# Four cross-attention layers on one core: narrower matmul tiles and one step order per engine

## The reference, cut to what matters

```python
# layer 0: 64 channels, 256 positions; no heads, 1x1 convolutions
Mn, Mm = Wn @ norm(x) + bn, Wm @ norm(ctx) + bm
A = softmax(Mn.T @ Mm)                    # 256 x 256 per batch
x = Wo @ ((Wl @ ctx + bl) @ A.T) + bo + x
# layers 1 and 2: 16 heads of 16, 64 queries and 64 keys per batch
a = layer_norm(ctx) * gamma + beta
Q, K, V = x @ Wq.T, a @ Wk.T, a @ Wv.T    # scores * 16 ** -0.5, masked
x = x + tanh(gate) * (softmax(Q K.T) V) @ Wo.T
# layer 3: one head of 256
x = x + alpha * (softmax((x Wq.T) (ctx Wk.T).T / 16) (ctx Wv.T)) @ Wo.T
```

## Time and profile before

| | us |
|---|---|
| median of 3 runs | 635.41 (635.09 to 635.55) |
| the profiled execution | 634.87 |
| its span | 633.1 |
| PE busy | 602.1 (95%) |
| ACT busy | 478.2 (76%) |
| DVE busy | 467.6 (74%) |
| POOL busy | 119.1 (19%) |

### The profile page before, as it was taken

The page is one execution under the profiler, slowest core; times in us unless marked ns, Lnnn a source line. Parts: engine busy times, 40 slices in busy tenths (PEclk is TensorE's granted clock), DMA queues, the critical chain, the costliest instruction groups (busy, mean ns, idle before and its releaser), DMA issues.

```text
span 633.1 us, 22469 instructions
## 1 busy us (share of the span) xinstructions
PE 602.1 (95%) x9203; PEld 540.0 (85%) x9203; DVE 467.6 (74%) x1036; ACT 478.2 (76%) x929; POOL 119.1 (19%) x136
## 2 busy tenths in 40 slices
PE   1899999999999999999999999999999999999995
PEld 1688998889898898989988898988989899889884
DVE  4866778686885869767786868858697677867474
ACT  0998779776885959857797768859598577977682
POOL 3602330107010060103301070100601033000000
PEclk9999999999999999999999999999999999999999
DMA  5420002010021000210020100210002100001001
GB/s 160 147 72 2 3 3 72 3 35 2 2 74 34 2 2 4 71 34 2 2 72 2 35 2 2 72 35 2 1 5 71 35 2 1 3 2 36 1 3 34
DMA packets 18486, 18.10 MB, mean 29 GB/s; under 512 B 1828, under 2 KB 18340, under 8 KB 18404
## 3 DMA queue, kind: packets, MB, share of 16 engines
q1 hardware_dynamic: 18024, 16.55, 8.2%
q0 software_dynamic: 320, 0.26, 0.2%
q10 hardware_dynamic: 60, 0.01, 0.0%
HBM read 12.63 MB, written 4.19 MB: 27 GB/s over the span
## 4 chain that ended last, share of the span: by engine, by line
PE 85%; ACT 5%; DVE 4%; issue 2%; DMA 1%; SPq 1%; DVEq 0%; POOL 0%; ACTq 0%; POOLq 0%
PE psum L401 13%; PE psum L403 10%; PE psum L402 10%; PE psum L641 10%; PE psum L716 10%; PE psum L662 8%; PE psum L709 4%; PE psum L629 4%; PE psum L507 2%; PE psum L467 2%; PE psum L532 2%; PE psum L515 2%; PE psum L546 1%; DMA mrow_u<-in_mask_dram 1%; PE psum L652 1%
## 5 line engine op out<-in xcount | busy, mean ns | idle before, releaser
L1046 DVE TENSOR_TENSOR shifted<-psum,negmax 128x512 f32<-128x512 f32 x128 | 88.5, 691 | 9.7 <-ACT work L842 4.8
L842 ACT ACTIVATE work<-shifted 128x512 f32<-128x512 f32 x128 | 78.1, 642 | 20.0 <-DVE shifted L1046 19.7
L1042 DVE TENSOR_REDUCE negmax<-psum 128x8 f32<-128x512 f32 x128 | 87.3, 682 | 4.7 <-PE psum L641 4.5
L856 ACT ACTIVATE work<-psum,group_mask 128x512 f32<-128x512 f32 x128 | 79.4, 697 | 2.1 <-PE psum L662 1.7
L641 PE MATMUL psum<-kbd,work 64*128 64x128 f32 x1024 | 69.7, 280 | 0.6 <-issue 0.4
L662 PE MATMUL psum<-const,work 64*128 64x64 f32 x1536 | 65.3, 225 | 4.3 <-ACT work L835 1.1
L716 PEld LDWEIGHTS psum<-v,work 128*64 128x64 f32 x2048 | 62.4, 138 | 6.8 <-issue 5.4
L662 PEld LDWEIGHTS psum<-const,work 64*128 64x128 f32 x1536 | 57.5, 139 | 10.6 <-issue 7.7
L641 PEld LDWEIGHTS psum<-kbd,work 64*128 64x128 f32 x1024 | 61.9, 188 | 5.2 <-issue 3.3
L716 PE MATMUL psum<-v,work 128*64 128x34 f32 x2048 | 66.1, 225 | 0.0
L803 ACT ACTIVATE work<-psum,const 128x512 f32<-128x512 f32 x64 | 40.5, 684 | 25.0 <-PE psum L403 24.8
(11 more groups left out here) (184 smaller groups left out, 1609.8 us busy)
## 6 DMA issues: line engine op xcount, KB each, us to landing
x_raw<-in_x_dram SPq DMA_DIRECT2D x8, 512.0 KB, 4.0
c_raw<-in_ctx_dram SPq DMA_DIRECT2D x8, 512.0 KB, 4.9
out_dram<-attn SPq DMA_DIRECT2D x16, 256.0 KB, 2.3
mrow_u<-in_mask_dram SPq DMA_DIRECT2D x8, 64.0 KB, 4.6
kbd<-in_L_xattn_Wq_dram SPq DMA_DIRECT2D x2, 256.0 KB, 6.7
kbd<-in_L_xattn_Wk_dram SPq DMA_DIRECT2D x2, 256.0 KB, 6.9
kbd<-in_L_xattn_Wv_dram SPq DMA_DIRECT2D x2, 256.0 KB, 7.0
kbd<-in_L_xattn_Wo_dram SPq DMA_DIRECT2D x2, 256.0 KB, 7.7
```

The lines of the kernel that those rows point to most:

```text
L842: act.activation(e, shifted[:, i % 2, :].rearrange("t (c k) -> t c k", c=NK), ACT.Exp).then_inc(exps, 1)
L856: act.activation(probsT[:, at, :], o[:], ACT.Copy, scale=group_mask[:, i:i + 1]).then_inc(free, 1)
L1042: dve.tensor_reduce(negmax[:, i % 2, :], sv, AX_X, ALU.max, negate=True).then_inc(rowmax, 1)
L1046: dve.tensor_tensor(shifted[:, i % 2, :].rearrange("t (j k) -> t j k", k=C), sv, negmax[:, i % 2, :].unsqueeze(2).broadcast_to([P, NJ, C]) ...
```

## The change

1. *Scores of layers 1 and 2 on 32x64 tiles.* Four steps are filled at once, one bank per strip of 32 partitions (`strips`): 32 matmuls of 32 rows by 64 columns over 128 moving columns. The queries are written once (`queries`), the keys still twice, scaled by `parity`. A step now holds one head pair per strip over four batches, so `T` reads the exponentials of four steps and waits for all four. `probs` has eight rows instead of four. `v2` holds a batch per entry, and each `V1` or `V2` is copied in four parts instead of two. Wo of layers 1 and 2 is no longer sorted by POOL, since the heads come out in order.
2. *Quarters.* `nT` (`mixed_quarters`) and `V0` (`value_quarters`) use 64x64 tiles, 32 matmuls each over 64 moving columns. `V0` is one block on PE with two copies on DVE.
3. *An order per engine.* `group_order` and `prologue_order` give way to tables per engine; a word like `S1.4-7` is steps 4 to 7. PE's order sets the banks.
4. *The next group's first queries.* `H.0`, `H.1`, `L.0`, `L.1` and `Q1.0` of the next group stand in the end of an iteration (and of the start). For that layer 0's pairs are taken in another order (`pair_at`), so that the first half of the state is whole after four of the eight `A0` steps.

```diff
-def group_order(front):
...
+PE_ORDER = """
+    V1.0 S1.0-3 V2.0 Q1.1 V3.0 S1.4-7 T1.0-1 K3.0 V1.1 A1.0-1 T1.2-3 AT1.0 K2.0 O1.0 A1.2-3 K2.1 AT1.1 Q2.0 O1.1 S2.0-3
+    xT.0-1 V2.1 V3.1 Q2.1 V0.0-1 Mn.0-1 T2.0 S2.4-7 T2.1 Mm.0-1 K3.1 A2.0-1 cT.0-1 T2.2 nT.0-1 AT2.0 T2.3 S0.0-3 A2.2-3
+    O2.0 AT2.1 K1.0 T0.0-3 S0.4-7 A0.0 S3.0 A0.1-3 T0.4-5 XN.0 O2.1 T3.0 T0.6-7 A0.4 S3.1 A0.5-7 XN.1 T3.1 Q1.0 K1.1
+    PV.0-1
+"""
+ACT_ORDER = """
+    V1.0 X1.0 V2.0 X1.1 SC.0 Q1.1 X1.2-3 V3.0 T1.0 X1.4-5 T1.1 X1.6 K3.0 X1.7 V1.1 AT1.0 T1.2-3 H.2 K2.0 AT1.1 K2.1 Q2.0
+    xT.0 H.3 X2.0-1 xT.1 V2.1 X2.2 Q2.1 X2.3 V3.1 Mn.0-1 T2.0-1 X2.4-5 Mm.0 K3.1 Mm.1 X2.6-7 cT.0-1 T2.2 nT.0-1 AT2.0 T2.3
+    X0.0-2 AT2.1 X0.3 K1.0 T0.0-3 X0.4-5 X3.0 X0.6 T0.4 X0.7 T0.5 XN.0 T3.0 T0.6-7 H.0 X3.1 T3.1 Q1.0 XN.1 H.1 K1.1
+"""
+DVE_ORDER = """
+    ST.0 S1.0-7 ST.1 A1.0-1 ST.2 AT1.0 O1.0 A1.2-3 L.2 ST.3 AT1.1 MV.0 O1.1 S2.0-1 L.3 S2.2-3 V0.0-1 Mn.0-1 S2.4-7 Mm.0-1
+    A2.0-1 cT.0-1 nT.0-1 AT2.0 S0.0-1 A2.2 S0.2 A2.3 S0.3 O2.0 AT2.1 S0.4-5 S3.0 S0.6 A0.1 S0.7 A0.3 O2.1 S3.1 L.0 X3.0
+    A0.5 X3.1 A0.7 PV.0-1 L.1
+"""
+PE_FIRST = """
+    MT.0 GT.0 xT.0-1 MS.0 Wq1.0 cT.0-1 Wq2.0 Wk1.0 Wo3T.0 Wv2.0 W0T.0 Wv1.0 M3.0 Wk2.0 Mn.0-1 Mm.0-1 VW3.0 W0.0 S0.0-3
+    V0.0-1 VB1.0 T0.0-1 Wo2.0 T0.2-3 A0.0-1 S0.4-5 nT.0-1 S0.6-7 A0.2 Wo1.0 A0.3 T0.4-5 K1.0 VB2.0 T0.6-7 K1.1 A0.4-7 Q1.0
+"""
...
             def front_halves(g, name, banks, signals):
...
+            def mixed_quarters(g, banks, signals):
+
+                pe.wait_ge(normed, 1 if g is None else g + 2)
+                pe.wait_ge(mix_ready, 1 if g is None else g + 2)
...
+                for n in range(NK * NP):
+                    k, p = n // NP, n % NP
+                    for f in range(2):
+                        for h in range(2):
+                            rows = slice(C * h, C * h + C)
+                            mm_ = pe.matmul(banks[h][C * f:C * f + C, C * n:C * n + C], c_norm[rows, p, P * k + C * f:P * k + C * f + C],
+                                            mix[rows, p, :], start=True, stop=True)
...
+            def value_quarters(banks, signals):
+
+                for p in range(NP):
+                    for s in range(2):
+                        for f in range(2):
+                            for h in range(2):
+                                rows = slice(C * h, C * h + C)
+                                mm_ = pe.matmul(banks[h][C * f:C * f + C, (2 * p + s) * C:(2 * p + s + 1) * C],
+                                                c_raw[rows, p, P * s + C * f:P * s + C * f + C], wv0[rows, rows], start=True, stop=True)
...
-                    for c in range(NK):
-                        for h in range(2):
-                            for to, done, rows in ((o, signal, slice(0, C)), (o2, signal2, slice(C, 2 * C))):
-                                dst = to[:, D * c:D * c + D].rearrange("t (r h s) -> t r h s", r=2, h=2)[:, :, h, :]
-                                mm_ = pe.matmul(dst, qe[rows, c, i + h].rearrange("p q t -> p (q t)"),
-                                                kbd[l - 1][rows, c, i + h], start=True, stop=True)
...
+                    strips = [(o, signal)] + [start_fill(g, ("S", l, i + r), last) for r in range(1, 4)]
+                    for n in range(2 * NK):
+                        p, k = n // NK, n % NK
+                        for r, (to, done) in enumerate(strips):
+                            rows = slice(32 * r, 32 * r + 32)
+                            for c in range(2):
+                                b = i + 2 * p + c
+                                mm_ = pe.matmul(to[C * c:C * c + C, P * n:P * n + P], queries[rows, k, C * b:C * b + C],
+                                                kbd[l - 1][rows, k, b].rearrange("p q s -> p (q s)"), start=True, stop=True)
...
-                    pe.wait_ge(exps, 18 * g + (8 * (l - 1) + 2 * i + 2))
...
+                    pe.wait_ge(exps, 18 * g + (8 * (l - 1) + 4 * (i // 2) + 4))
...
-                    for q in range(2):
-                        ins = act.activation(qe[:, :, 4 * i:4 * i + 4, q, :], o[:].rearrange("p (k b t) -> p k b t", k=NK, t=C),
-                                             ACT.Identity, scale=parity[:, q:q + 1])
-                    ins.then_inc(free, 1)
+                    act.activation(queries[:, :, HALF * i:HALF * i + HALF], o[:].rearrange("p (k t) -> p k t", k=NK),
+                                   ACT.Copy).then_inc(free, 1)
```

More of the change, by code:

```diff
@@ new lines, with steps @@
+NEXT = ("xT", "cT", "nT", "Mn", "Mm", "V0", "K1", "ST", "MV")
+def steps(table, front):
+    out = []
+    for word in table.split():
+        name, index = word.split(".")
+        first, last = index.split("-") if "-" in index else (index, index)
+        attends = name[0] in "SXTA" and name[1:].isdigit()
+        if not front and (name in NEXT or attends and name[1:] == "0"):
+            continue
+        for i in range(int(first), int(last) + 1):
+            if not front and (name, i) in AHEAD:
+                continue
+            if attends:
+                out.append((name[0], int(name[1:]), i))
+            elif name in ("H", "L", "SC", "ST", "MV", "WB", "NB", "TG", "NM", "ON", "KB", "OB"):
+                out.append((name, i))
+            else:
+                out.append(("P", name, i))
+    return out
@@ L139, in fills_of @@
+    SPLIT_WEIGHTS = [s for s in ACT_PROLOGUE if s[0] == "P" and s not in EARLY and (s[1][0] == "W" and s[1][1] in "qkv" or s[1] in ("Wo1", "Wo2", "M3", "VW3"))]
     def fills_of(order):
@@ L263, in build @@
         beta_row = scratch[:, 11:13]
-        v2 = [sb(f"v2_{l}", [P, NP, NH, 2, VW]) for l in (1, 2)]
-        qe = work[:, 8:12, :].rearrange("p a b -> p (a b)").rearrange("p (k b q t) -> p k b q t", k=NK, b=GB, q=2)
+        v2 = [sb(f"v2_{l}", [P, GB, NJ, 2, VW]) for l in (1, 2)]
+        queries = work[:, 12:14, :]
         negmax = sb("negmax", [P, 2, NJ])
@@ L511, in proj_step @@
                     return
-                elif name == "V0":
-                    for q in range(2):
-                        for s in range(2):
-                            mm_ = pe.matmul(o[:, (2 * q + s) * P:(2 * q + s + 1) * P], c_raw[:, 2 * i + q, P * s:P * s + P],
-                                            wv0[:], start=True, stop=True)
                 elif name in ("K1", "K2", "K3"):
@@ L714, in weighted_step @@
                 for j in range(NJ):
[L715 to L717 removed]
+                    for c in range(2):
+                        mm_ = pe.matmul(o[C * c:C * c + C, 2 * VW * j:2 * VW * (j + 1)], probsT[:, at + c, C * j:C * j + C],
+                                        v2[l - 1][:, 2 * i + c, j].rearrange("k q v -> k (q v)"), start=True, stop=True)
                 mm_.then_inc(signal, 1)
             def iteration(g, last):
[L721 removed]
+                for step in (PE_LAST if last else PE_STEPS):
                     if step[0] == "P":
@@ L732, in _ @@
                 pe.sem_inc(freed[bk], PER[bk])
-            for step in PROLOGUE:
-                if step in FRONT:
+            for step in PE_PROLOGUE:
+                if step in EARLY:
                     proj_step(None, step, False)
@@ L816, in state_high @@
                 if n < 2:
-                    act.wait_ge(state_ready, 2 * g + (n + 1))
+                    bk, nth = fill(g, ("A", 0, 4 * n + 2), last)
+                    act.wait_ge(freed[bk], released(bk, nth))
                 else:
@@ L888, in iteration @@
             def iteration(g, last):
-                for step in (LAST_ORDER if last else ORDER):
-                    if step[0] == "E" or step[0] == "P" and ("E",) + step[1:] not in ORDER:
-                        proj_step(g, ("P",) + step[1:], last)
+                for step in (ACT_LAST if last else ACT_STEPS):
+                    if step[0] == "P":
+                        proj_step(g, step, last)
                     elif step[0] == "SC":
@@ L1150, in iteration @@
             def iteration(g, last):
-                for step in (LAST_ORDER if last else ORDER):
-                    if step[0] == "E" or step[0] == "P" and ("E",) + step[1:] not in ORDER:
-                        proj_step(g, ("P",) + step[1:], last)
+                for step in (DVE_LAST if last else DVE_STEPS):
+                    if step[0] == "P":
+                        proj_step(g, step, last)
                     elif step[0] == "S":
@@ L1183, in _ @@
             dve.tensor_copy(scale_row[0:3, :], gate_in[:].broadcast_to([3, P])).then_inc(gates_spread, 1)
-            for step in PROLOGUE:
+            for step in DVE_PROLOGUE:
                 if step in FRONT:
```

284 lines of the change are left out of this document (124 added, 160 removed).

## The result

The changed kernel takes **655.1 us** (median of 4 runs, 654.0 to 659.1) against 635.5 before: a ratio of 1.032, 95% interval 1.029 to 1.035. It is 3.1% slower where I had forecast 1.4% faster, and 29 us off. The profiled execution took 654.9 us with a span of 653.1.

What follows compares the result with a forecast made beforehand. TensorE was taken to bound the groups: 73.85 us each, less 0.85, seven times (-6.0), and -3.0 at the ends, take the span from 633.07 to 624.1. Plus 1.8 around it: 626 us, range 614 to 633.5, chance 0.52.

Steps and rivals of the forecast that it cites:

- the start put at 0: Stretch before the first group: Q1.0 adds 1.4 us, two quartered blocks save 1.7; taken as 0, between -3 and +3.
- the clock left full behind the wait: PE's work after its wait before Mn in each group was priced at full clock, with no added time.
- the list of waits: New waits per group: Mn 4.0 us, T1.0 0.7, O1.0 and O1.1 0.3 together, T2.2 and AT2.0 0.2 each; sum 5.4.
- the last group's second half at 34: Last group's second half, a chain of 32.06 us before, was put at 34, with V3.1 added and VectorE idling.
- rival C: Idle PE slows in each group: 3 us of work doubled, priced 7 x 1.5 more, 636 us; chance 0.06.
- the wait for POOL: PE's Mn block in each group waits for POOL's last normalising instruction, 12.07 us after the moments: 4.0 us, seven times.
- rival D: More small waits than counted, some 1 us per group: 633 us; chance 0.12, within two us of before.
- T1.0, O1 and T2.2: Smaller new PE waits per group: T1.0 0.7 us, O1.0 and O1.1 0.3 together, T2.2 0.2.
- the quarters' missing 0.45: Layer 0's mixing and values on 64x64 tiles were to save 0.85 and 0.84 us of PE per group.
- the tile model: Tiles cost 0.83 ns per column plus 5 ns and overlap across rows or columns; a scores block takes 0.90 us.
- B: Matmul records bound by issue at 29 ns: scores, mixing and values blocks take 1.86 us; 654 us; chance 0.12, halves included.
- A's arithmetic: Rival in which the Mn wait does not bite: groups 69.7 us, VectorE's scores binding instead, 603 us; chance 0.18.

Runs made afterwards that it cites:

- wait_filled: The changed kernel with seven needless full-array fp32 matmuls on PE ahead of its wait for the normalised rows: 648.3 us, ratio 1.018.
- queries_early: moments_early with Q1.1 ahead of V2.0 on PE and ScalarE, and K3.0 between S1.4-7 and T1.0: 617.8 us, ratio 0.972.
- moments_early: The changed kernel with VectorE's fourth statistics step and the moments moved ahead of O1.0 in its order: 623.7 us, ratio 0.982.
- start_scalar_fed: queries_early with a start laid for ScalarE (Wk1, TG, Wv1 before normalisation) and PE's Wo3T and W0 ahead of Mn: 615.6 us, ratio 0.969.
- start_as_before: moments_early with the start's three orders laid as in the kernel before the change: 620.5 us, ratio 0.976.
- last_scores_first: moments_early with, in the last group alone, K3.1 and S2.4-7 right behind Q2.1, ahead of T2.0: 627.0 us, ratio 0.986.
- moments_between: The changed kernel with the moments between A1.3 and L.2 on VectorE, 2.4 us earlier: 632.6 us, ratio 0.996.
- before_moments_late: The kernel before the change, with only the moments moved 14.3 us later, between L.3 and layer 2's first scores: 657.6 us, ratio 1.034.

## Why the prediction was wrong

**No single step carries the 29 us.** The groups have 15.9 of them, the start 9.0, the last group 4.1. The steps that failed are the start put at 0, the clock left full behind the wait, the copy of Q1.1 left out of the list of waits, and the last group's second half at 34. The start is the largest of them, and any one put right alone would have moved the forecast of 626 to 635 at most.

**The step on the clock: that PE keeps it behind the wait (rival C, given 6 in 100, priced at 1.5 us a group).** The forecast had the wait for POOL nearly: 4.0 us predicted, 3.5 measured, seven times, for the reason given (12.07 us from the moments to the last x_norm; here 238.2 to 250.2). I then let work behind it run at full clock, because the pause was "shorter than those in the start (over 4.5 us)". That was no evidence on either side: no row showed fast work behind a pause of 3 us. And the 24 slow transposes of the earlier trace rows run from 17.4 to 26.1 us, where the trace holds no clock record: its first begins at 26.3 us, and the 1.00 printed ahead of that is not a reading. C's own price fits 3 us spent at half clock, not 3 us of work doubled, which would be 3 us a group. wait_filled puts the clock at 1.1 us a group and, with the rest of what it changes, 7 us in all (655.1 to 648.3). Forecast and this together would still have been only 633.

**Small waits and the other order terms (rival D).** Of 2.3 us per group above the forecast's 73.0, the clock has 1.1. Q1.1's copy has 0.7 (queries_early): I had listed T1.0, O1 and T2.2, not S1.4-7, whose queries ScalarE copies only behind V2.0's four copies and an exponential. The Mn wait was 0.5 smaller. The rest is 1.0: the quarters' missing 0.45, and some 0.5 that no run isolates (small waits such as that for mn_lo, 0.5 once a group in moments_early).

**The start, taken at 0 with bounds of 3, was 9.** The step by which two quartered blocks pay for Q1.0 looked at PE alone in the earlier trace rows, where ScalarE has 25.45 of 25.93 us busy. It was the fuller engine, and the sum gave nothing for the time in which it goes unfed. Wo3T on PE ahead of five weight transposes, which I named as the price, does not give the size: ScalarE lost 4.6 us of the ten from 20 to 30. start_scalar_fed, which feeds ScalarE first, begins its first group 4.9 us sooner; start_as_before, with the three orders of the kernel before, 1 us sooner, but at half clock for 10.2 us. That the start is set by how early ScalarE is fed is the best reading of these runs and not proven by them, since the clock moved along with it. Of the 9 us, 4.9 are thus regained by order, 1.5 is Q1.0 itself and 2.6 stay open.

**The last group, -3 predicted, was +1.** First half 28.1 us up to its scores of layer 2 (587.78 to 615.84) against 27.2; second half 37.3 against 34. The wait of PE for the fourth exponential that I had foreseen is there (1.95 us ahead of T2.0); a second one like it, 2.31 us, stands ahead of T2.2 at 632.54 us, and behind that the clock halves for 3.4 us, where the block of 64 weighted sums takes 3.13 us instead of 2.06. The clock stands at 0.93 over the group. Taking the first wait away brought nothing (last_scores_first). Whether the second wait or the half clock makes most of these 4 us stays open.

**Right.** The wait for POOL, its place, size and cause: moments_early takes it away, and 31 us with it and the half clock. Right too was the tile model. B is refuted: 64 records of a scores block go by in 1.13 us with the changes of shape, 18 ns each, far below the 29 ns of the earlier trace rows, so eight 32x64 tiles do overlap. Saved per pair of blocks 0.85 of the 0.90 forecast. The Trainium skill (TensorE: Matmul & The Clock Gate, "Wait — 56ns, not 53.3ns?") states a floor of about 25 ns from start to start; the measurement differs from it, and decides. The same page (Part 1: The HAM clock gate) has an idle TensorE fall back to 1.2 GHz, and there the traces agree in six groups of seven: 0.51 granted behind 3.51 us of idleness, but 1.00 behind 3.54 us in the first. A's arithmetic, that without the wait a group takes 69.7, came out 1.0 short: moments_early has 70.7, and the 70.0 of queries_early needed another wait taken away.

## What to carry to other kernels

An instruction of no size of its own can head a long chain on an idle engine: when an order is changed, measure from each such head to its last reader, and move the head up into the nearest idle stretch of its engine. When the engine that sets the pace must wait, price the work behind it at the lower clock, even where one row shows the full clock behind a wait as long: here the same wait gave both. And in a stretch with several full engines, look at the fullest one first, however little it is named in the diff.

## What was not expected of the hardware

- The half clock is not a fixed price of a wait. Idle 1.1 us (moments_between): clock 1.00 in all seven groups. Idle 2.1 us (before_moments_late): halved in five groups of seven. Idle 3.5 us (the changed kernel): halved in six of seven, not in the first, and for twice as long in the second.
- It need not begin with the wait: in the third group of the changed kernel the first 16 records after it still ran at 1.00, the next 92 at 0.51. In the second group the clock fell 1.1 us before PE resumed, and the first 16 were slow already.
- Work that is thrown away can make a kernel faster: 3.3 us of needless matmuls in each wait gained 7 us (655.1 to 648.3).
